# A graph kernel with VectorE's preparation of the next chunk laid out in another order over the tiles

## What is computed

```python
dx = jnp.maximum(edge_attr[:, 0], EPS)
inv_dx = 1.0 / dx
slope_e = edge_attr[:, 1] * inv_dx
diff = (u[dst] - u[src]) * inv_dx[:, None]
d1 = segment_sum(diff, dst) - segment_sum(diff, src)
S = segment_sum(broadcast(slope_e), dst)
u_next = u - clip(dt) * (u * d1 + g * S)
```

## Time and profile before

| what | us |
|---|---|
| median of 3 runs (4681.98 to 4691.01) | 4688.31 |
| the profiled execution | 4681.29 |
| its span, first to last instruction | 4679.5 |
| TensorE matmuls busy (96%) | 4485.3 |
| VectorE busy (82%) | 3823.7 |
| GpSimd busy (77%) | 3597.0 |
| ScalarE busy (31%) | 1430.6 |
| granted TensorE clock, mean share of full speed | 0.996 |

### The profile page before, as it was taken

How to read it: one execution, slowest core, us unless ns; L and a number is a source line. 1 busy time by engine, 2 the same in 40 slices (tenths; PEclk the granted TensorE clock), 3 DMA queues, 4 the chain that set the end, 5 groups by cost and what they waited for, 6 DMA issues and landing times. The chain is left out here.

```text
span 4679.5 us, 90558 instructions
## 1 busy us (share of the span) xinstructions
PE 4485.3 (96%) x31379; PEld 2683.7 (57%) x31380; DVE 3823.7 (82%) x8582; ACT 1430.6 (31%) x1014; POOL 3597.0 (77%) x3133
## 2 busy tenths in 40 slices
PE   3999999999999999999999999999999999999996
PEld 2666555555555555555555555555555555555554
DVE  6888888878888788888888888887888878888886
ACT  4332233222332223322332223322332223322220
POOL 7777777777777777777777777777777777777770
PEclk9999999999999999999999999999999999999998
DMA  3111111111111111111111111111111111111110
GB/s 91 34 34 43 34 33 34 40 37 34 33 34 41 36 34 33 34 43 34 34 34 34 43 34 34 33 42 34 34 34 34 43 34 34 34 34 42 34 22 7
DMA packets 212186, 168.11 MB, mean 36 GB/s; under 512 B 126538, under 2 KB 195662, under 8 KB 211912
## 3 DMA queue, kind: packets, MB, share of 16 engines
q1 hardware_dynamic: 111734, 139.99, 9.3%
q0 software_dynamic: 100000, 25.80, 6.2%
q10 hardware_dynamic: 428, 2.01, 0.1%
HBM read 164.74 MB, written 2.81 MB: 36 GB/s over the span
## 5 line engine op out<-in xcount | busy, mean ns | idle before, releaser
L584 PE MATMUL ps_src<-hi_hot,spread 128*128 128x391 bf16 x25000 | 4309.4, 329 | 91.4 <-DVE hi_hot L858 91.3
L379 POOL DMA_INDIRECT x_src<-in_x_dram,src_i x3125 | 3592.0, 1149 | 955.9 <-issue 861.2
L584 PEld LDWEIGHTS ps_src<-hi_hot,spread 128*128 128x128 f16 x25000 | 2185.7, 97 | 1659.1 <-DVE hi_hot L858 199.4
L858 DVE TENSOR_SCALAR hi_hot<-col_h,hi_f,scale 128x1564 bf16<-128x1564 f16 x3125 | 2127.4, 697 | 205.9 <-PE ps_src L584 205.8
L790 DVE TENSOR_TENSOR spread<-lo_rows,halves 128x640 f16<-128x640 f16 x1250 | 554.4, 485 | 82.1 <-issue 80.0
L525 PE MATMUL ps_x<-xwin,node_of_dst 128*128 128x48 bf16 x3125 | 575.0, 187 | 11.5 <-ACT node_of_dst L467 11.5
L442 ACT CAST parts<-pay 128x425 bf16<-128x425 f32 x125 | 72.5, 580 | 1642.5 <-DVE pay L750 1642.5
L525 PEld LDWEIGHTS ps_x<-xwin,node_of_dst 128*128 128x128 bf16 x3125 | 298.9, 97 | 228.7 <-issue 12.2
L457 ACT CAST parts<-left 128x400 bf16<-128x400 f32 x125 | 71.6, 573 | 1041.2 <-DVE left L847 1041.2
L465 ACT ACTIVATE node_of_dst<-rel_all,row_neg 128x3200 bf16<-128x3200 f16 x125 | 369.8, 2959 | 6.6 <-DMA rel_all<-rel_d 6.6
L467 ACT ACTIVATE node_of_dst<-node_of_dst,ones 128x3200 bf16<-128x3200 bf16 x125 | 370.3, 2963 | 4.1
(11 more groups left out here) (110 smaller groups left out, 1006.1 us busy)
## 6 DMA issues: line engine op xcount, KB each, us to landing
rel_all<-rel_d SPq DMA_DIRECT2D x125, 800.0 KB
x_src<-in_x_dram,src_i POOLq DMA_INDIRECT x3125
a<-in_edge_attr_dram SPq DMA_DIRECT2D x125, 200.0 KB
a<-in_edge_attr_dram SPq DMA_DIRECT2D x125, 25.0 KB, 1.8
src_i<-in_src_dram SPq DMA_DIRECT2D x125, 12.5 KB, 1.6
dst_i<-in_dst_dram SPq DMA_DIRECT2D x125, 12.5 KB, 1.7
xwin<-xparts_d SPq DMA_DIRECT2D x125, 12.0 KB, 1.7
dst_sum<-in_dst_dram SPq DMA_DIRECT2D x1, 1562.5 KB
```

The lines of the kernel that those rows point to most:

```text
L379: nc.gpsimd.indirect_dma_start(x_src[:, b, j * F:(j + 1) * F], None, x[:, :], bass.IndirectOffsetOnAxis(ap=src_i[:, b, j:j + 1], axis=0)). ...
L584: last = nc.tensor.matmul(ps_src[:, q, 0:HB], spread[:, b, j, k, :, :].rearrange("p l f -> p (l f)"), hi_hot[:, slot(b, j), q * HB:(q + 1) ...
L858: v.tensor_scalar(hi_hot[:, slot(b, j), :], col_h[:, :], hi_f[:, b, j:j + 1], scale[:, b, j:j + 1], ALU.is_equal, ALU.mult).then_inc(hi_ho ...
```

## The change

Only the table and two numbers change. The `spread` pieces stand one behind each of the tiles 12 to 21, where two stood behind each of 8 to 12. The `dst_rel` and `dst_hot` pieces come first, in tiles 1 to 5, one `dst_hot` a tile. `diff` moves from tile 1 to tile 5, and the pieces that follow it move by four tiles with it. `slope` stands at tile 22, `window` and `attr_left` at tile 23, `attr_parts` at 24. The row matmuls start at tile 4 and end at tile 16 (8 and 20 before); the sums stand behind tile 11 (7 before). The new file is one line longer, so that a line of after is that of before plus one from here on.

```diff
-        SUM_AT, ROWS_AT = 7, 8
-        PIECES = {0: ["x_of_dst"], 1: ["diff"], 2: ["pay"], 3: ["scale"], 4: ["scaled"], 5: ["left"], 6: ["parts"],
-                  8: ["spread"] * 2, 9: ["spread"] * 2, 10: ["spread"] * 2, 11: ["spread"] * 2, 12: ["spread"] * 2,
...
+        SUM_AT, ROWS_AT = 11, 4
+        PIECES = {0: ["x_of_dst"], 1: ["dst_rel", "dst_hot"], 2: ["dst_hot"], 3: ["dst_hot"], 4: ["dst_hot"], 5: ["dst_hot", "diff"],
```

More of the change, by code:

```diff
@@ L256, in gnn_kernel @@
         TROW, TCOL = TAIL // P, TAIL % P
-        SUM_AT, ROWS_AT = 7, 8
-        PIECES = {0: ["x_of_dst"], 1: ["diff"], 2: ["pay"], 3: ["scale"], 4: ["scaled"], 5: ["left"], 6: ["parts"],
-                  8: ["spread"] * 2, 9: ["spread"] * 2, 10: ["spread"] * 2, 11: ["spread"] * 2, 12: ["spread"] * 2,
-                  13: ["dst_rel"], 14: ["dst_hot"] * 2, 15: ["dst_hot"] * 2, 16: ["dst_hot", "slope"], 17: ["window"], 19: ["attr_left"], 21: ["attr_parts"]}
+        SUM_AT, ROWS_AT = 11, 4
+        PIECES = {0: ["x_of_dst"], 1: ["dst_rel", "dst_hot"], 2: ["dst_hot"], 3: ["dst_hot"], 4: ["dst_hot"], 5: ["dst_hot", "diff"],
+                  6: ["pay"], 7: ["scale"], 8: ["scaled"], 9: ["left"], 10: ["parts"],
+                  12: ["spread"], 13: ["spread"], 14: ["spread"], 15: ["spread"], 16: ["spread"], 17: ["spread"], 18: ["spread"],
+                  19: ["spread"], 20: ["spread"], 21: ["spread"], 22: ["slope"], 23: ["window", "attr_left"], 24: ["attr_parts"]}
         FIRST_HALF = ["dst_rel", "dst_hot", "slope", "attr_left", "attr_parts"]
```

## The result

| | before | after |
|---|---|---|
| median of 5 runs each, us | 4688.31 (4681.98 to 4691.01) | 4565.59 (4565.30 to 4566.12) |
| span of the profiled execution, us | 4679.5 | 4563.7 |
| granted TensorE clock, mean | 0.996 | 0.994 |

The ratio is 0.9737, 95% interval 0.9723 to 0.9750: faster by 2.6%. The forecast was 4967, and the range began at 4820. What came is the case of rival D, which was priced at 4562.

What follows compares the result with a forecast made beforehand. GpSimd's gathers were taken as the bound, 36.5 us a chunk. 3.0 - 0.3 - 0.35 = +2.35 a chunk over about 121 chunks: 4681.3 + 284 - 5 = 4960, plus 7 for timed runs: 4967 us; range 4820 to 5070.

Steps and rivals of the forecast that it cites:

- rival D: Faster: spaced pieces leave gathers more often free, GpSimd drops under TensorE's 35.5 us a chunk; 4562 us; chance 0.06.
- Step 1: Spread, ten tiles with one piece for five with two: each gather thrown back to 1.70 us, +3.0 us a chunk.
- One-hots don't: Gathers beside VectorE: tensor_scalar one-hots do not throw a gather back, only tensor_tensor pieces do; no delay from one-hots alone.
- the half microsecond: A VectorE piece running at a gather's start, or about half a microsecond in, throws it to 0.90 us after the piece.
- Step 2: One-hots of dst one at a time in tiles 1 to 5: 0.94 us of delay against 1.21, -0.3 a chunk.
- Step 4: window and attr_left share tile 23: one gather caught, about 0.3 us, for 0.66 extra before; -0.35 a chunk.
- Steps 3, 5 and 6: scaled, left, parts at tiles 8 to 10; row matmuls in tiles 4 to 16; sums behind tile 11: 0 each.
- Step 7: Difference at tile 5: four tiles less remain for TensorE behind the last gather, -5.4 us, once.

Runs made afterwards that it cites:

- before_22_gathers: Kernel before with three of the 25 gathers of each chunk left out from the fourth chunk on: 4562.88 us, ratio 0.9731.
- port_bench: Bench without the kernel's computation: 24 gathers beside each repeated VectorE pattern; one-hot and one spread piece gave gathers of 0.95 us or 1.69 to 1.70.
- after_spread_pairs_2: Changed kernel with its ten spread pieces put back in pairs (tiles 12 to 16): 4615.09 us, ratio 0.9839 of the kernel before.
- after_26_gathers: Changed kernel with one gather more a chunk, a repeat whose rows nothing reads: 4683.61 us, ratio 0.9988 of the kernel before.
- before_spread_single: Kernel before with spread pieces and dst one-hots one a tile, window and attr_left sharing tile 23: 5187.61 us, ratio 1.0511, on the slow chip.

## Why the prediction was wrong

- **The bound** was read rightly. GpSimd's gathers set the time, TensorE needed 35.5 a chunk (measured: 35.4), and before_22_gathers shows both.
- **Step 1, the spread pieces, is the step that failed**: "So each gather takes 1.70 and they come every 2.00 us", +3.0 us a chunk. Measured over the stretch it is -0.5 (0.86 to 0.38 us of delay; -0.6 with 26 gathers). The 1.70 rhythm exists, and port_bench measured it to the hundredth. But there is a second one that keeps itself up as well, and the kernel is nearly always in that one: of 1178 gathers beside the spread, 4 take over 1.6 us. The working put every gather 0.20 into a one-hot and let only the gather give way. In truth VectorE gives way too: a piece that comes due behind a one-hot in GpSimd's 0.30 us between two gathers is held to the start of the next. That fixes VectorE's period at 1.25, and from then on nothing disturbs a gather. The whole chunk's delay is 25 x (1.102 - 0.944) = 3.9 us where it was 5.2, and not 5.2 + 2.35.
- The sign was in the rows. In the earlier trace rows the three one-hots from 30.29 take 2.06 us, and three of 0.60 with the overlap of 0.08 make 1.88. The missing 0.18 lies ahead of the gather's start at 31.01: the first one-hot is due to end at 30.89, and the second begins at 31.01. I used the row to show that one-hots don't delay a gather, and did not look at what the gather does to the one-hots.
- **"One-hots don't"** is wrong as a rule. The gathers at 2007.32 and 393.90 begin in a one-hot and end 0.89 to 0.90 behind its end, and so do nearly all that begin 0.27 to 0.57 into one. Also wrong is the half microsecond: the piece at 2006.60 begins 0.53 into the gather of 2006.07, which takes its 0.94. I had weighed a rule of the Trainium skill ("SBUF — State Buffer", SBUF: two separate sides), by which the port pair is an exclusive lock between VectorE and GpSimd, taken for the whole instruction, and set it aside for the one-hots; I had also left out that it counts two SBUF inputs only against a GpSimd operation that reads SBUF. Both engines being held in turn fits a lock. One that is held for the whole instruction doesn't fit: in step, a gather of 0.94 us runs beside a piece and half of a one-hot, and in the stretch of one-hots alone it takes 0.94 to 0.95 too, from the second gather on (there, two one-hots take 1.25 us in place of 1.20, in step with the gathers).
- **Step 2** (dst one-hots, -0.3) did not come: with the difference, the delay there was 1.63 before and is 1.69 in after_spread_pairs_2, 1.59 with 26 gathers. **Step 4** (window and attr_left, -0.35) came, and larger: 0.72 before, 0.21 and 0.11 in these two. It is what the -0.5 us a chunk of after_spread_pairs_2 consists of.
- **Steps 3, 5 and 6** (0) stood: the delay at scaled, left and parts is 2.03 before and 2.05 with 26 gathers, and TensorE has no wait at the row matmuls or the sums that reaches the time, since it is busy for 4000 of 4000 us.
- **Step 7** (-5.4 at the end) holds for a kernel that GpSimd bounds: from the start of the last gather to the end of the span it is 130.2 us before, 125.3 in after_spread_pairs_2 and 124.7 in after_26_gathers. In the changed kernel TensorE is the bound, and it is 146.9.
- **Rival D** had the outcome and the number (4562 against 4565.59), through its second half: GpSimd under TensorE's need. Its condition, a gather in the one-piece rhythm that costs under 0.1, is what the rows in step show (0.94 and 0.95; over the whole spread stretch 0.38 us for 10.4 gathers, 0.04 each). I gave it 0.06 because "nothing in the rows shows so little".

## What to carry to other kernels

Where two engines hinder each other, look in the trace for stretched instructions on both, and work out the common rhythm with both giving way: it can lock in a state in which the engine that matters loses nothing, and the other pays from what it has to spare. A periodic pattern may have several such states, so an estimate from one starting phase is worth little; a bench of the two instruction streams alone, run from several phases, shows them in half a millisecond. It doesn't tell which of them the kernel is in: for that, count the starting phases in the kernel's own trace. Where several moves are made at once, add up the delay by the place where it arises; the time alone is cut off at the next bound and hides who gave what. And where an engine is the bound by 3% only, removing gathers (a kernel that leaves work out) tells in one run how far down the next bound is.

## What the runs showed of the hardware

- A gather issued by GpSimd and a stream of VectorE's one-hot and one spread piece run either at 0.95 us every 1.25 or at 1.70 every 2.00, and stay so while nothing disturbs them (17 gathers and 13 in a row in the benches). A gather that begins 0.27 to 0.57 us into a one-hot is let go behind the one-hot (932 of 933 in six kernels), one that begins 0.14 to 0.26 into it mostly behind the piece (239 of 289).
- VectorE is held as well: what follows a one-hot and comes due in the 0.30 us between two gathers starts with the next gather. What follows a piece does not wait (all 1061 such one-hots of the two main traces against none of 1073 pieces).
- GpSimd paused for 3.06, 3.08 and 3.25 us in the benches with nothing in the trace that it waits for, and behind each pause the gathers ran in the slow rhythm. What causes such a pause stays open.
- None of the three kinds of VectorE instruction that were repeated alone (one-hot, spread piece, dst one-hot) slows the gathers (0.945 to 0.955 us). Two pieces behind a one-hot cost 0.15 to 0.19 us a gather, an f32 product into strided places 0.9 when thrown.
- One chip ran the kernel before in 4934 us, where it took 4688 to 4690 in the other groups, and on it before_spread_single was 5.1% slower at a clock of 0.963, not 2.7% faster. The changed kernel itself was not run there. Whether the change gains on such a chip is not known.
